# GpSimd takes six of the sixteen products with B, at the head of a tile, in a Mamba and mixture-of-experts block

## The chip, the cores and the metric

One core of a Trainium2 chip. The metric is the device time of one execution in microseconds. The kernel before took 1973.01 us (median of 3 runs, 1966.05 to 1973.41).

## The reference

The input is four images of 256 channels and 24 x 24 pixels. Two layers follow one another. Each is x = x + mamba(norm(x)), then t = t + experts(norm(t)), where the experts are a top-2 mixture of eight. The change lies in the Mamba part alone, which is the same in both layers:

```python
u, z = split(seq @ in_proj_w.T)                     # 128 channels each
u  = silu(causal_conv4(u) + conv_b)
dt, B, C = split(u @ x_proj_w.T, [4, 20])           # B and C: 16 states each
dt = softplus(dt @ dt_proj_w.T + dt_proj_b)
h  = exp(dt * A) * h + (dt * u) * B                 # per channel and state, step by step along the sequence
y  = sum_over_states(h * C) + u * D
out = (y * silu(z)) @ out_proj_w.T
```

A sequence has 2304 pixels and a leading token.

## The kernel before

The Mamba stage works on 24 tiles of T = 384 steps of the sequence per layer, six to an image. 128 channels times 16 states are 2048 rows of 384. They are held as 16 slices `c` of 128 partitions. A slice holds 32 channels of four states (partition group n of 32 and k = c // 4 pick the state, g = c % 4 the quarter of the channels). The code's N is 16 and its Q is 4. The prediction calls slice c "scan c" and "decay c", and the four slices of one k "group k".

Per tile the five engines do this:

- SyncE (`send`) stores the tile's B and C rows (`L_bc`, 20 rows) and dt and dt*u (`L_dw`) to memory and reads them back spread over the partitions: `L_dwq` in four DMAs (L738), `L_cbq` in four DMAs (L743). Of the five rows of 384 in a partition of `L_cbq`, four are C for the groups 0 to 3, and the fifth is B for group 3.
- ScalarE (`decay`, L492) makes exp(dt*A) for each slice into one of three PSUM banks, so decay c can start when scan c-3 is done. In between it makes the next tiles' silus (L454, L460, each pair between two loads of the function table, L536 and L540) and the steps of softplus (L213 to L232) two tiles ahead.
- VectorE makes the product (dt*u)*B for two slices at once (`times_b`, L574), from `L_dwq` and a spread of B that TensorE has put into PSUM, and runs the scans (`scan`, L587, one hardware scan of 384 steps per slice). It also makes dt*u (L595), the gate (L602) and the residual (L607), and after each second tile copies the last state (L649).
- GpSimd multiplies h by C, a whole group at a time (`times_c`, L669, called hc below), and makes the product with B for group 3, from `L_cbq`, in two instructions (L678). It also makes one subtraction of the softplus (L661).
- TensorE sums hc over the states (L364), spreads B for groups 0 to 2 (L354), and makes the projections: u and z (L323, L330), dt (L340), B and C (L336), the output (L371).

The order on each engine is the order in which the code is written; there is no scheduler. Every engine works through its own list and waits on semaphores. On TensorE a tile's list is: the three adding matmuls of softplus (L344, L348, L350) and z for the next tile; sum of hc 3 of the tile before; u for the tile after next (L323); spread of B for group 2; u*D (L358); sum of hc 0; spread of B for the next tile; dt and B, C projections for the tile after next; sum of hc 1; output of the tile before; spread of B; sum of hc 2. On ScalarE the first two softplus steps for the tile after next (L213, L216) stand between decay 10 and decay 11, and wait for the projection L340. `L_hc` has room for two groups.

`tile_pairs` writes out the first and last pair of tiles and loops over the pairs between. A pair has an even tile (r = 0) and an odd one (r = 1).

Of the kernel before, what the change touches and what calls it, by code (L numbers as in the profile page):

```python
# [16 lines left out]
ALU = mybir.AluOpType  # L17
# [3 lines left out]
P = 128  # L21
# [5 lines left out]
T = 4 * PT  # L27
NT = TOK // PT
TPB = PIX // PT
N = 16  # L30
TAPS = 4
E = 8
Q = 4
QW = P // Q
QR = Q + 1
DA_RING = 3
# [200 lines left out]
def mamba(nc, m, L, wp):  # L237
# [14 lines left out]
    with ExitStack() as ctx:  # L252
        new = ctx.enter_context(semaphores(nc))

        def sb(name, shape, dt=F32):
            return ctx.enter_context(nc.sbuf_tensor(f"{L}_{name}", shape, dt))
# [24 lines left out]
        dwq = sb("dwq", [P, 2, Q, 2, T])  # L281
        dbu = sb("dbu", [P, 6, T])
        dbp = sb("dbp", [P, Q, T])
        h = sb("h", [P, N, T])
# [30 lines left out]
        def _(pe):  # L315
# [36 lines left out]
            def spread_b(t, r, k):  # L352
                wait(pe, sem["dbu"], 6 * t + 2 * k - 2)
                nc.tensor.matmul(b_ps(r, k), w_b[:, k, :], u[:, r, :], start=True, stop=True).then_inc(sem["b"], 1)  # L354
# [208 lines left out]
        def _(dve):  # L563
            def times_b(t, r, p, k, i):
                dve.wait_ge(sem["b"], 3 * t + k + 1)
                if k == 0 and i == 0:
                    dve.wait_ge(s_dw[r], 64 * (p + 1))
                q = 2 * k + i
                if q >= 3:
                    dve.wait_ge(sem["scan"], t * N + 2 * q - 4)  # L570
                else:
                    wait(dve, sem["scan"], (t - 1) * N + 2 * q + 8)
                at = 2 * (q % 3)
                nc.vector.tensor_tensor(dbu[:, at:at + 2, :], dwq[:, r, 2 * i:2 * i + 2, 1, :], spread(b_ps(r, k)),  # L574
                                        ALU.mult).then_inc(sem["dbu"], 1)

            def scan(t, c, slot):
                k, g = c // Q, c % Q
                dve.wait_ge(sem["da"], t * N + c + 1)
                if k < Q - 1:  # L580
                    dve.wait_ge(sem["dbu"], 6 * t + c // 2 + 1)
                else:
                    dve.wait_ge(sem["dbu_p"], 2 * t + g // 2 + 1)
                wait(dve, sem["hc"], Q * (t - 1) + k + 1)
                first = h[:, c, T - 1:T] if slot is None else carry[:, slot, c:c + 1] if isinstance(slot, int) \
                    else carry[:, bass.ds(slot, 1), c:c + 1].rearrange("p a n -> p (a n)")
                nc.vector.tensor_tensor_scan(h[:, c, :], da(t % 2 if isinstance(t, int) else int(slot is None), c),  # L587
                                             dbu[:, c % 6, :] if k < Q - 1 else dbp[:, g, :], first, ALU.mult, ALU.add
                                             ).then_inc(sem["scan"], 1)
# [35 lines left out]
            def tile(t, r, p, slot, last):  # L625
                for j in range(N // 2):
                    k, i = (j + 1) // 2, (j + 1) % 2
                    if k < Q - 1:
                        times_b(t, r, p, k, i)
                    elif j == N // 2 - 1 and not last:  # L630
                        times_b(t + 1, 1 - r, p + r, 0, 0)
                    scan(t, 2 * j, slot)
                    scan(t, 2 * j + 1, slot)
                    if j == 1 and not last:
                        times_u(t + 1, 1 - r, [(s_dw_row[r], 16 * (p + 1))])
                    if not (isinstance(t, int) and t == 0):
# [21 lines left out]
        def _(pool):  # L658
# [13 lines left out]

            def times_b(t, r, p, i):
                if i == 0:
                    pool.wait_ge(s_cb[r], 64 * (p + 1))
                    pool.wait_ge(s_dw[r], 64 * (p + 1))
                    wait(pool, sem["scan"], t * N)
                nc.gpsimd.tensor_tensor(dbp[:, 2 * i:2 * i + 2, :], dwq[:, r, 2 * i:2 * i + 2, 1, :],  # L678
                                        spread(cbq[:, r, Q, :]), ALU.mult).then_inc(sem["dbu_p"], 1)

# [18 lines left out]

            def tile(t, r, p, last):  # L700
                for k in range(Q):
                    times_c(t, r, p, k)
                    if k < 2:
                        times_b(t, r, p, k)
                    if k == 2 and not last:
                        lost(t + 2)
# [10 lines left out]
        def _(sp_):  # L717
# [4 lines left out]
            def send(t, r, p):  # L722
                gone, there = count(64 * p), count(16 * (p + 1))
                bc_out, dt_out, w = count(t + 1), count(t + 1), count(t + 1)
                decayed, driven, mixed, driven_p = count((t - 1) * N), count((t - 1) * 6), count((t - 1) * Q), count((t - 1) * 2)
                sp_.wait_ge(sem["bc_out"], bc_out)
# [625 lines left out]
def pack(np, g):  # L1352
# [71 lines left out]
```

## Time and profile before

| | |
|---|---|
| median of 3 runs | 1973.01 us |
| profiled execution | 1973.6 us |
| its span | 1971.8 us |
| TensorE / VectorE / GpSimd / ScalarE busy | 73% / 69% / 58% / 47% of the span |
| mean granted clock of TensorE | 0.878 of full |

The profile is of one execution. Times are in microseconds from the start of its span. In a row of the timeline the first number is the start, the second how long the instructions of the row lasted from first start to last end; a number in brackets is the idle time ahead of it on its engine and what ended it. Matmul ends are modelled. Since an instruction's write-back lies beside the start of the next, the step from one start to the next is a little shorter than the duration. PE is TensorE, DVE VectorE, ACT ScalarE, POOL GpSimd, SPq SyncE's DMA queue. The scans of the first Mamba stage run from about 50 to 550, those of the second from about 1060 to 1600. The rows come from one even tile (413.90 to 436.3) and the odd one behind it (436.3 to 457.7), which have no irregular wait.

### The profile page before, as it was taken

Reading aid. Unit: us, or ns where it says so; the run is one execution under the profiler, and the core shown is the slowest. Engines: PE = TensorE matmul, PEld = TensorE weight load, DVE = VectorE, ACT = ScalarE, POOL = GpSimd, SP = SyncE. Lnnn points to the kernel's source line nnn. Section 1 sums busy time; section 2 is a strip of 40 time slices with the busy share of each in tenths; the row PEclk is TensorE's granted clock in tenths of the full one; section 3 lists DMA queues with packets and bytes.
Section 4 is the critical chain, followed back from the end, with each engine's and each line's share of the span. In section 5 each row is a group of like instructions: output and inputs, shape, how many; then the busy total and the mean of one; then the engine's idle time right before and its main releaser. Section 6 shows DMA issues by size and latency. Waiting matters only on the chain. (4 is left out here: it accounts for less than half of the span.)

```text
span 1971.8 us, 28551 instructions
## 1 busy us (share of the span) xinstructions
PE 1445.4 (73%) x7776; PEld 980.9 (50%) x7777; DVE 1359.6 (69%) x1913; ACT 928.1 (47%) x1695; POOL 1138.6 (58%) x788
## 2 busy tenths in 40 slices
PE   6666766667656599999956766666667662799993
PEld 4333333333314499999834333333333222799992
DVE  2899999999995422222143999999999967444443
ACT  6666677667743011111136666677666731011111
POOL 0687788888880244444302888888878850355540
PEclk9889898998968699999968788998998866899996
DMA  3655566555638110111034565566555634111114
GB/s 110 147 135 121 129 144 146 125 126 134 145 79 354 54 41 32 38 37 36 26 126 98 129 138 121 129 143 139 134 121 135 148 136 188 38 48 48 47 41 152
DMA packets 75964, 217.61 MB, mean 110 GB/s; under 512 B 11856, under 2 KB 27408, under 8 KB 72592
## 3 DMA queue, kind: packets, MB, share of 16 engines
q1 hardware_dynamic: 67664, 194.53, 38.9%
q0 software_dynamic: 8256, 22.56, 3.5%
q8 instruction: 20, 0.33, 0.1%
q14 instruction: 24, 0.20, 0.0%
HBM read 178.34 MB, written 38.70 MB: 110 GB/s over the span
## 5 line engine op out<-in xcount | busy, mean ns | idle before, releaser
L669 POOL TENSOR_TENSOR L_hc<-L_h,L_cbq 128x1536 f32<-128x1536 f32 x192 | 660.1, 3438 | 210.6 <-DVE L_h L587 207.5
L492 ACT ACTIVATE ps<-L_dwq,L_negA 128x384 f32<-128x384 f32 x768 | 426.7, 574 | 227.4 <-DVE L_h L587 215.5
L364 PE MATMUL ps<-L_hc,same 128*32 128x384 f32 x1536 | 190.0, 571 | 238.9 <-POOL L_hc L669 238.9
L574 DVE TENSOR_TENSOR L_dbu<-L_dwq,ps 128x768 f32<-128x768 f32 x288 | 270.7, 941 | 29.4 <-DVE L_carry L649 13.1
L587 DVE TENSOR_TENSOR_SCAN L_h<-ps,L_h,L_dbu 128x384 f32<-128x384 f32 x288 | 275.0, 1002 | 12.9 <-ACT ps L492 12.8
L587 DVE TENSOR_TENSOR_SCAN L_h<-ps,L_carry,L_dbu 128x384 f32<-128x384 f32 x288 | 274.2, 1001 | 6.5 <-DVE L_dbu L574 4.7
L364 PEld LDWEIGHTS ps<-L_hc,same 128*32 128x32 f32 x1536 | 31.5, 113 | 358.2 <-POOL L_hc L669 324.3
L1151 DVE COPY Xn<-L_w 128x2048 f32 x86 | 107.6, 1253 | 117.1 <-PE ps L1101 108.3
L1134 ACT ACTIVATE L0e_hT<-ps 128x512 f32<-128x512 f32 x86 | 51.3, 597 | 267.2 <-PE ps L1101 267.2
L678 POOL TENSOR_TENSOR L_dbp<-L_dwq,L_cbq 128x768 f32<-128x768 f32 x96 | 175.1, 1824 | 0.0
L323 PE MATMUL ps<-Xn,L_fold 128*128 (+1 forms) x480 | 103.3, 368 | 89.2 <-DVE L_dw L595 89.2
L1101 PE MATMUL ps<-L0e_xT,Xn 128*128 128x128 f32 x1376 | 159.1, 277 | 3.2 <-DVE Xn L1151 3.2
L1101 PEld LDWEIGHTS ps<-L0e_xT,Xn 128*128 128x128 f32 x1376 | 158.8, 194 | 4.7 <-issue 3.6
L1101 PE MATMUL ps<-L1e_xT,Xn 128*128 128x128 f32 x1376 | 159.1, 277 | 2.6 <-DVE Xn L1151 2.6
L1101 PEld LDWEIGHTS ps<-L1e_xT,Xn 128*128 128x128 f32 x1376 | 158.3, 194 | 4.6 <-issue 3.2
L1116 PE MATMUL ps<-L_w,L0e_hT 128*128 x688 | 152.3, 380 | 0.9 <-ACT L0e_hT L1134 0.9
L323 PEld LDWEIGHTS ps<-Xn,L_fold 128*128 128x128 f32 x480 | 87.7, 211 | 120.0 <-issue 102.5
L354 PE MATMUL ps<-L_u,L_wp 128*128 128x384 f32 x288 | 141.9, 579 | 0.0
L1116 PEld LDWEIGHTS ps<-L_w,L0e_hT 128*128 128x128 f32 x688 | 129.4, 191 | 17.3 <-issue 1.1
L1134 ACT ACTIVATE L1e_gl<-ps 128x512 f32<-128x512 f32 x43 | 25.7, 597 | 217.7 <-PE ps L1101 217.7
L661 POOL TENSOR_TENSOR L_sp_a<-L_sp_e,L_sp_g 128x384 f32<-128x384 f32 x48 | 48.3, 1006 | 123.1 <-ACT L_sp_g L228 123.1
L1039 POOL TENSOR_TENSOR L0e_give_done<-ones 128x1 f32<-128x1 f32 x44 | 8.5, 192 | 164.1 <-DVE L0e_yt L1173 162.3
(278 smaller groups left out, 2301.4 us busy)
## 6 DMA issues: line engine op xcount, KB each, us to landing
L_dwq<-dw_rows SPq DMA_DIRECT2D x192, 384.0 KB, 6.2
L_cbq<-cb_rows SPq DMA_DIRECT2D x192, 240.0 KB, 9.9
dw_rows<-L_dw SPq DMA_DIRECT2D x48, 384.0 KB, 2.3
L_w<-in_up SPq DMA_DIRECT2D x16, 1024.0 KB, 11.7
L_w<-in_down SPq DMA_DIRECT2D x8, 1024.0 KB, 26.6
tok_rows<-Xn SPq DMA_DIRECT2D x6, 768.0 KB, 13.1
L0s_got<-results SPq DMA_DIRECT2D x18, 256.0 KB, 2.9
L1s_got<-results SPq DMA_DIRECT2D x18, 256.0 KB, 3.5
```

What stands on the lines that cost most here:

```text
L323: mm = nc.tensor.matmul(ua_ps[:, j * (T // 2):(j + 1) * (T // 2)], fold[:, g, :], column(t, img, back), start=(k in (0, 2)), stop=(k in (1 ...
L354: nc.tensor.matmul(b_ps(r, k), w_b[:, k, :], u[:, r, :], start=True, stop=True).then_inc(sem["b"], 1)
L364: mm = nc.tensor.matmul(y_ps[g * QW:(g + 1) * QW, :], same[:, 0:QW], hc[:, (k % 2) * Q + g, :], start=False, stop=(k == Q - 1))
L492: nc.scalar.activation(da(r, c), dwq[:, r, c % Q, 0, :], ACT.Exp, scale=negA[:, 0, c:c + 1]).then_inc(sem["da"], 1)
L574: nc.vector.tensor_tensor(dbu[:, at:at + 2, :], dwq[:, r, 2 * i:2 * i + 2, 1, :], spread(b_ps(r, k)), ALU.mult).then_inc(sem["dbu"], 1)
L587: nc.vector.tensor_tensor_scan(h[:, c, :], da(t % 2 if isinstance(t, int) else int(slot is None), c), dbu[:, c % 6, :] if k < Q - 1 else d ...
L669: nc.gpsimd.tensor_tensor(hc[:, at:at + Q, :], h[:, Q * k:Q * k + Q, :], cbq[:, r, k, :].unsqueeze(1).to_broadcast([P, Q, T]), ALU.mult).t ...
L678: nc.gpsimd.tensor_tensor(dbp[:, 2 * i:2 * i + 2, :], dwq[:, r, 2 * i:2 * i + 2, 1, :], spread(cbq[:, r, Q, :]), ALU.mult).then_inc(sem["d ...
L1101: mm = nc.tensor.matmul(ps[:, h * NBH + b, (f % BF) * TS:(f % BF + 1) * TS], w1_t[:, h, i, f * P:(f + 1) * P], xT[:, r, i, h, :], start=(i ...
L1116: mm = nc.tensor.matmul(ps[:, 7, h * D:(h + 1) * D], hT[:, r, h, f, :], w2[:, bass.ds(e[h], 1), f, :].rearrange("p e d -> p (e d)"), start ...
L1134: nc.scalar.activation(dst, ps[:, h * NBH + b, :], ACT.Silu if gated else ACT.Gelu).then_inc(sem["act"], 1)
L1151: nc.vector.tensor_copy(w1_t[:, h].rearrange("p i f -> p (i f)"), w1[:, bass.ds(e, 1)].rearrange("p e i f -> p (e i f)")).then_inc(sem["st ...
```

## The change

GpSimd makes six products with B instead of four: those of the slices 10 to 15. B for group 2 is sent through the spread by DMA too, so `L_cbq` has six rows, `L_bc` 24. VectorE makes the ten others in five instructions, which stand where they stood; the sixth, for the slices 10 and 11, is gone. GpSimd's products are one of 768 columns (slices 10 and 11) and one of 1536 (12 to 15), and both stand at the head of the tile, ahead of `times_c` for group 0; before, there were two of 768 behind groups 0 and 1. `L_dbu` has ten rows instead of six and is no longer used in rotation, `L_dbp` has six instead of four.

```diff
-QR = Q + 1
+QR = Q + 2
...
-        dbu = sb("dbu", [P, 6, T])
-        dbp = sb("dbp", [P, Q, T])
+        dbu = sb("dbu", [P, 10, T])
+        dbp = sb("dbp", [P, 6, T])
...
             def spread_b(t, r, k):
-                wait(pe, sem["dbu"], 6 * t + 2 * k - 2)
+                wait(pe, sem["dbu"], 5 * t + (-1, 0, 2)[k])
...
-                q = 2 * k + i
-                if q >= 3:
-                    dve.wait_ge(sem["scan"], t * N + 2 * q - 4)
-                else:
-                    wait(dve, sem["scan"], (t - 1) * N + 2 * q + 8)
-                at = 2 * (q % 3)
+                at = 4 * k + 2 * i
+                wait(dve, sem["scan"], (t - 1) * N + at + 2)
...
-                if k < Q - 1:
-                    dve.wait_ge(sem["dbu"], 6 * t + c // 2 + 1)
+                if c < 10:
+                    dve.wait_ge(sem["dbu"], 5 * t + c // 2 + 1)
                 else:
-                    dve.wait_ge(sem["dbu_p"], 2 * t + g // 2 + 1)
+                    dve.wait_ge(sem["dbu_p"], 2 * t + (1 if c < 12 else 2))
...
             def tile(t, r, p, slot, last):
                 for j in range(N // 2):
                     k, i = (j + 1) // 2, (j + 1) % 2
-                    if k < Q - 1:
+                    if 2 * k + i < 5:
                         times_b(t, r, p, k, i)
...
-            def times_b(t, r, p, i):
-                if i == 0:
-                    pool.wait_ge(s_cb[r], 64 * (p + 1))
-                    pool.wait_ge(s_dw[r], 64 * (p + 1))
-                    wait(pool, sem["scan"], t * N)
-                nc.gpsimd.tensor_tensor(dbp[:, 2 * i:2 * i + 2, :], dwq[:, r, 2 * i:2 * i + 2, 1, :],
-                                        spread(cbq[:, r, Q, :]), ALU.mult).then_inc(sem["dbu_p"], 1)
+            def times_b2(t, r, p):
+                pool.wait_ge(s_cb[r], 64 * (p + 1))
+                pool.wait_ge(s_dw[r], 64 * (p + 1))
+                wait(pool, sem["scan"], (t - 1) * N + 12)
+                nc.gpsimd.tensor_tensor(dbp[:, 0:2, :], dwq[:, r, 2:4, 1, :], spread(cbq[:, r, Q + 1, :]), ALU.mult
+                                        ).then_inc(sem["dbu_p"], 1)
+
+            def times_b3(t, r):
+                wait(pool, sem["scan"], t * N)
+                nc.gpsimd.tensor_tensor(dbp[:, 2:6, :], dwq[:, r, :, 1, :],
+                                        cbq[:, r, Q, :].unsqueeze(1).to_broadcast([P, Q, T]), ALU.mult
+                                        ).then_inc(sem["dbu_p"], 1)
...
             def tile(t, r, p, last):
+                times_b2(t, r, p)
+                times_b3(t, r)
                 for k in range(Q):
                     times_c(t, r, p, k)
-                    if k < 2:
-                        times_b(t, r, p, k)
                     if k == 2 and not last:
                         lost(t + 2)
```

GpSimd's list for the first two tiles of a layer, before. `L_dbp` is the product with B, `L_hc` that with C, `L_sp_a` the subtraction:

```order
15 L669 TENSOR_TENSOR L_hc<-L_h,L_cbq 128x1536 [waits L0_scan,L0_cb_spread0]
16 L678 TENSOR_TENSOR L_dbp<-L_dwq,L_cbq 128x768 [waits L0_dw_spread0,L0_cb_spread0]
17 L669 TENSOR_TENSOR L_hc<-L_h,L_cbq 128x1536 [waits L0_scan]
18 L678 TENSOR_TENSOR L_dbp<-L_dwq,L_cbq 128x768
19 L669 TENSOR_TENSOR L_hc<-L_h,L_cbq 128x1536 [waits L0_scan,L0_y]
20 L661 TENSOR_TENSOR L_sp_a<-L_sp_e,L_sp_g 128x384 [waits L0_g]
21 L669 TENSOR_TENSOR L_hc<-L_h,L_cbq 128x1536 [waits L0_scan,L0_y]
22 L669 TENSOR_TENSOR L_hc<-L_h,L_cbq 128x1536 [waits L0_scan,L0_y,L0_cb_spread1]
23 L678 TENSOR_TENSOR L_dbp<-L_dwq,L_cbq 128x768 [waits L0_scan,L0_dw_spread1,L0_cb_spread1]
24 L669 TENSOR_TENSOR L_hc<-L_h,L_cbq 128x1536 [waits L0_scan,L0_y]
```

and the same place now (L665 was L669, L673 and L678 are the new products):

```order
15 L673 TENSOR_TENSOR L_dbp<-L_dwq,L_cbq 128x768 [waits L0_dw_spread0,L0_cb_spread0]
16 L678 TENSOR_TENSOR L_dbp<-L_dwq,L_cbq 128x1536
17 L665 TENSOR_TENSOR L_hc<-L_h,L_cbq 128x1536 [waits L0_scan,L0_cb_spread0]
18 L665 TENSOR_TENSOR L_hc<-L_h,L_cbq 128x1536 [waits L0_scan]
19 L665 TENSOR_TENSOR L_hc<-L_h,L_cbq 128x1536 [waits L0_scan,L0_y]
20 L657 TENSOR_TENSOR L_sp_a<-L_sp_e,L_sp_g 128x384 [waits L0_g]
21 L665 TENSOR_TENSOR L_hc<-L_h,L_cbq 128x1536 [waits L0_scan,L0_y]
22 L673 TENSOR_TENSOR L_dbp<-L_dwq,L_cbq 128x768 [waits L0_scan,L0_dw_spread1,L0_cb_spread1]
23 L678 TENSOR_TENSOR L_dbp<-L_dwq,L_cbq 128x1536 [waits L0_scan]
24 L665 TENSOR_TENSOR L_hc<-L_h,L_cbq 128x1536 [waits L0_scan,L0_y,L0_cb_spread1]
```

Both products moved ahead of hc 0 of their tile, and so directly behind hc 3 of the tile before.

VectorE's list from the gate (L602) of an odd tile to the copy of the last state, before (`L_yz` is the gate, a scan is printed as SCALAR_TENSOR_TENSOR):

```order
54 L602 TENSOR_TENSOR L_yz<-L_zs,ps 128x384
55 L574 TENSOR_TENSOR L_dbu<-L_dwq,ps 128x768
56 L587 SCALAR_TENSOR_TENSOR L_h<-ps,L_h,L_dbu 128x384 x2
57 L574 TENSOR_TENSOR L_dbu<-L_dwq,ps 128x768
58 L587 SCALAR_TENSOR_TENSOR L_h<-ps,L_h,L_dbu 128x384 x4
59 L587 SCALAR_TENSOR_TENSOR L_h<-ps,L_h,L_dbp 128x384 x2
60 L607 TENSOR_TENSOR X<-X,ps 128x2x96
```

and now:

```order
52 L598 TENSOR_TENSOR L_yz<-L_zs,ps 128x384
53 L570 TENSOR_TENSOR L_dbu<-L_dwq,ps 128x768
54 L583 SCALAR_TENSOR_TENSOR L_h<-ps,L_h,L_dbu 128x384 x4
55 L583 SCALAR_TENSOR_TENSOR L_h<-ps,L_h,L_dbp 128x384 x4
56 L603 TENSOR_TENSOR X<-X,ps 128x2x96
```

The product between scan 7 and scan 8 is gone, and the scans 10 and 11 read GpSimd's buffer. The lists of TensorE and ScalarE keep their order; the projection and the copy of B and C have 24 rows instead of 20.

## Rows read from the trace of the kernel before

**Rows 1.** The page: busy us of each engine, share of the span, instructions.

```profile
PE 1445.4 (73%) x7776; PEld 980.9 (50%) x7777; DVE 1359.6 (69%) x1913; ACT 928.1 (47%) x1695; POOL 1138.6 (58%) x788
```

**Rows 2.** Windows of two tiles: us, busy PE, PEld, DVE, ACT, POOL, clock, DMA.

```profile
413.90:436.30 22.40, 16.57 (x73) 8.12 (x70) 21.41 (x28) 16.19 (x29) 18.24 (x7) 0.86 0.58 133
436.30:457.70 21.40, 13.27 (x69) 6.33 (x69) 21.15 (x26) 15.22 (x27) 18.26 (x7) 1.00 0.62 139
```

**Rows 3.** Waits of VectorE, whole span: us in total, times, longest.

```profile
DVE L_h L587 <- ACT ps L492: 14.6, 31, 1.9
...
DVE L_dbu L574 <- PE ps L354: 10.3, 7, 2.1
```

**Rows 4.** Timeline of VectorE in the odd tile: start, us, instruction.

```profile
442.97 1.92 DVE L587 TENSOR_TENSOR_SCAN L_h<-ps,L_h,L_dbu 128x384 f32<-128x384 f32 x2
...
445.25 0.94 DVE L574 TENSOR_TENSOR L_dbu<-L_dwq,ps 128x768 f32<-128x768 f32 x1
446.12 1.91 DVE L587 TENSOR_TENSOR_SCAN L_h<-ps,L_h,L_dbu 128x384 f32<-128x384 f32 x2
447.95 0.93 DVE L574 TENSOR_TENSOR L_dbu<-L_dwq,ps 128x768 f32<-128x768 f32 x1
449.13 3.74 DVE L587 TENSOR_TENSOR_SCAN L_h<-ps,L_h,L_dbu 128x384 f32<-128x384 f32 x4 [0.25 <-ACT ps L492]
452.84 1.92 DVE L587 TENSOR_TENSOR_SCAN L_h<-ps,L_h,L_dbp 128x384 f32<-128x384 f32 x2
```

**Rows 5.** Timeline of ScalarE in the odd tile.

```profile
444.01 0.58 ACT L492 ACTIVATE ps<-L_dwq,L_negA 128x384 f32<-128x384 f32 x1 [1.71 <-DVE L_h L587]
444.62 1.28 ACT L536 ACT_TABLE_LOAD   x1
...
448.34 1.59 ACT L492 ACTIVATE ps<-L_dwq,L_negA 128x384 f32<-128x384 f32 x3
449.87 0.56 ACT L213 ACTIVATE L_sp_a<-ps,L_wp 128x384 f32<-128x384 f32 x1
...
452.07 0.57 ACT L492 ACTIVATE ps<-L_dwq,L_negA 128x384 f32<-128x384 f32 x1
```

**Rows 6.** Timeline of GpSimd in the odd tile.

```profile
436.40 3.44 POOL L669 TENSOR_TENSOR L_hc<-L_h,L_cbq 128x1536 f32<-128x1536 f32 x1 [0.17 <-DVE L_h L587]
441.76 3.45 POOL L669 TENSOR_TENSOR L_hc<-L_h,L_cbq 128x1536 f32<-128x1536 f32 x1 [1.92 <-DVE L_h L587]
445.16 1.84 POOL L678 TENSOR_TENSOR L_dbp<-L_dwq,L_cbq 128x768 f32<-128x768 f32 x1
...
451.51 1.84 POOL L678 TENSOR_TENSOR L_dbp<-L_dwq,L_cbq 128x768 f32<-128x768 f32 x1
453.30 3.43 POOL L669 TENSOR_TENSOR L_hc<-L_h,L_cbq 128x1536 f32<-128x1536 f32 x1
```

**Rows 7.** Timeline of TensorE in the odd tile.

```profile
446.23 0.85 PE L364 MATMUL ps<-L_hc,same 128*32 128x384 f32 x8
447.01 0.91 PE L354 MATMUL ps<-L_u,L_wp 128*128 128x384 f32 x2
447.76 0.81 PE L340 MATMUL ps<-L_u,L_w_dt 128*128 128x384 f32 x2
...
451.60 0.85 PE L364 MATMUL ps<-L_hc,same 128*32 128x384 f32 x8 [2.28 <-POOL L_hc L669]
```

**Rows 8.** Timeline of GpSimd and ScalarE in the even tile.

```profile
413.98 3.43 POOL L669 TENSOR_TENSOR L_hc<-L_h,L_cbq 128x1536 f32<-128x1536 f32 x1
...
428.36 0.56 ACT L213 ACTIVATE L_sp_a<-ps,L_wp 128x384 f32<-128x384 f32 x1
```

**Rows 9.** Timeline of TensorE in another tile, as its clock falls.

```profile
1382.69 1.40 PE L364 MATMUL ps<-L_hc,same 128*32 128x384 f32 x8 [2.80 <-POOL L_hc L669]
1384.03 1.65 PE L344 MATMUL ps<-L_sp_r,ident 128*128 128x384 f32 x2
```

**Rows 10.** The page: DMA issues, KB each, median us from issue to landing.

```profile
L_cbq<-cb_rows SPq DMA_DIRECT2D x192, 240.0 KB, 9.9
```

**Rows 11.** Timeline of SyncE's queue in the odd tile.

```profile
446.39 1.77 SPq L743 DMA_DIRECT2D L_cbq<-cb_rows  x4
```

More of the change, by code:

```diff
@@ L577, in scan @@
             def scan(t, c, slot):
-                k, g = c // Q, c % Q
+                k = c // Q
                 dve.wait_ge(sem["da"], t * N + c + 1)
-                if k < Q - 1:
-                    dve.wait_ge(sem["dbu"], 6 * t + c // 2 + 1)
+                if c < 10:
+                    dve.wait_ge(sem["dbu"], 5 * t + c // 2 + 1)
                 else:
-                    dve.wait_ge(sem["dbu_p"], 2 * t + g // 2 + 1)
+                    dve.wait_ge(sem["dbu_p"], 2 * t + (1 if c < 12 else 2))
                 wait(dve, sem["hc"], Q * (t - 1) + k + 1)
@@ L587, in scan @@
                 nc.vector.tensor_tensor_scan(h[:, c, :], da(t % 2 if isinstance(t, int) else int(slot is None), c),
-                                             dbu[:, c % 6, :] if k < Q - 1 else dbp[:, g, :], first, ALU.mult, ALU.add
+                                             dbu[:, c, :] if c < 10 else dbp[:, c - 10, :], first, ALU.mult, ALU.add
                                              ).then_inc(sem["scan"], 1)
@@ L724, in send @@
                 bc_out, dt_out, w = count(t + 1), count(t + 1), count(t + 1)
-                decayed, driven, mixed, driven_p = count((t - 1) * N), count((t - 1) * 6), count((t - 1) * Q), count((t - 1) * 2)
+                decayed, driven, mixed, driven_p = count((t - 1) * N), count((t - 1) * 5), count((t - 1) * Q), count((t - 1) * 2)
                 sp_.wait_ge(sem["bc_out"], bc_out)
@@ L1370, in pack @@
     state = g("x_proj_w")[4:].reshape(2, Q, Q, P)
-    put("bc", np.concatenate([state[1].transpose(1, 0, 2), state[0, Q - 1][:, None]], 1).reshape(Q * QR, P).T)
+    put("bc", np.concatenate([state[1].transpose(1, 0, 2), state[0, Q - 1][:, None], state[0, Q - 2][:, None]], 1).reshape(Q * QR, P).T)
     put("brep", np.repeat(state[0].reshape(N, P), QW, 0).T)
```

## The prediction

> **What bounds the kernel now.** I first read the busy shares of the page and then two neighbouring tiles of the stretch that the diff touches. VectorE (DVE) is busy 69% of the span and GpSimd (POOL) 58% [rows 1]; inside a tile of the state scan VectorE has work for 21.4 of 22.4 us (an even tile) or 21.2 of 21.4 us (an odd one) [rows 2]. That looks like a stage in which each VectorE instruction costs its full time. The list of waits corrects this: in the scans VectorE waits 31 times for ScalarE (ACT) and 7 times in the products for TensorE (PE), 14.6 and 10.3 us together [rows 3]. So I laid the instructions of one odd tile side by side, engine by engine [rows 4 to 7]. I call its states 0 to 15, "scan 8" the scan of state 8, "decay 8" ScalarE's exp for it, "group k" the four states 4k to 4k+3, and "hc k" GpSimd's product of h with C for group k.
>
> What is to be seen there: scan 8 starts at 449.13, and the product that stands ahead of it started at 447.95 and lasts 0.93. Instructions of VectorE that need not wait follow a product after about 0.86 us (scans 6 and 7 start 0.87 after their product started at 445.25), so scan 8 could have started at 448.81; the row puts 0.25 us on ScalarE [rows 4]. On ScalarE decay 7 starts at 444.01, when scan 4 has freed its bank, and then follow without a gap two table loads of 1.28 with two silus between them, and decay 8 at 448.34 [rows 5]. Scan 4 started at 442.97. From scan 4 to scan 8 there are therefore 6.16 us that belong to ScalarE, whatever VectorE does between. After scan 8 ScalarE has no gap either: the first softplus step (L213) at 449.87, decay 12 from 452.07 to 452.64, and scan 12 starts at 452.84, 0.20 after it.
>
> **The change on VectorE: one product less, worth nothing.** The removed instruction is the product of 128x768 just ahead of scan 8, 48 in all, 0.86 us of its time each. Were all of it on the path, 48 x 0.86 = 41.3 us would go. But VectorE then stands ready for scan 8 at 447.95, and decay 8 still comes at 448.34, so scan 8 starts at 449.13 as before: the wait grows from 0.3 to 1.2 us. The even tile has the same order on ScalarE. I take 0, with 0 and 41.3 as the two ends; 0 is what the nearest rows show.
>
> The Trainium skill ("Perfetto Trace Analysis", Identifying the Most-Contended Engine) tells to take the engine with the highest occupancy as the bottleneck and work on it first. By that rule the 41.3 us would come off. The row above speaks against it for this place; the rule stands as a rival below.
>
> **The change on GpSimd.** Before, its order in a tile was hc 0, product of 768, hc 1, product of 768, hc 2, subtraction (L661), hc 3. Now it is product of 768, product of 1536, hc 0, hc 1, hc 2, subtraction, hc 3. The product of 1536 is not in the trace: hc has its shape, with the same broadcast second input, and goes on after 3.40 us (441.76 to 445.16); two products of 768 would be 2 x 1.79 = 3.58. I take 3.40. Its work in a tile grows by 3.40 - 1.79 = 1.61 us to about 19.9 us [rows 2, 6], still under a tile's 21.4. What matters is where it stands. hc 3 of the tile before can start only when scan 15 is done, and both products now come behind it and ahead of hc 0. Odd tile: hc 3 starts at 436.40, + 3.40 + 1.79 + 3.40 puts hc 0 at 444.99, and its 3.45 end it at 448.44. Before it ended at 445.21 [rows 6]. Both new waits of the products (the spreads, and the scans of the last tile) are past by then, so the order alone makes this delay.
>
> **Who waits for hc 0.** TensorE's queue is in order. The sum over hc 0 (L364) stands ahead of the spread of B for the next tile, of the projection for dt (L340) and the one for B and C of the tile after. Before, that sum started at 446.23 and the projection for dt was done at 447.76 + 0.81 = 448.57, 2.34 us later [rows 7]. Now it starts at 448.44 + 0.05 = 448.49 and the projection is done at 450.83. ScalarE had L213 at 449.87 in its order, 1.30 us of cover; now it starts at 450.87, and that is 1.00 us late. Behind it on ScalarE are decays 11 to 15, and VectorE waits for those. The whole run to decay 12 moves by 1.00, so scan 12 comes at 453.84. VectorE alone is there earlier: scans 8 to 11 end at 452.84 if nothing holds them [rows 4], and scan 11 is held by less than the 1.0 us, as decay 11 had some lead. So ScalarE decides, and the end of the tile, and with it the next hc 3, is 1.00 later. Odd tile: 21.40 + 1.00 = 22.40 us.
>
> Even tile: hc 3 starts at 413.98 [rows 8], + 12.04 is 426.02, the sum at 426.07, the projection done at 428.41, L213 at 428.45 instead of 428.36: 0.09 late. It has the carry's copy at its head, which is why the same chain just fits. Both kinds of tile end up bound by one loop: scan 15, hc 3, two products, hc 0, sum, spread, projection, softplus, decay 12, scan 12 to 15.
>
> Sum: the chain exists where a tile t+2 follows, 11 odd and 11 even tiles in each of two layers. 22 x 1.00 = +22.0; 22 x 0.09 = +2.0. Against it: of the waits in [rows 3] about 22 x 0.25 = 5.5 us are the regular one before scan 8; the other 19.4 come in single tiles, which the list doesn't place. Where they fall in an odd tile, up to 1.0 us each is swallowed by the new wait; hc 2, no longer behind a product (451.51 to 453.30), starts when scan 11 ends and saves the even tiles up to 0.3 each. I take -5 for both (0 to -12).
>
> **TensorE's clock.** It was granted 0.86 in the even tile and 1.00 in the odd one [rows 2]; 0.86 is a mix of 2.4 and 1.2 GHz. Groups of matmuls at the higher level last 0.85 (L364) and 0.91 (L354, like L344 two passes of 384 columns) [rows 7]; at the lower 1.40 and 1.65 [rows 9]. If the chain ran at the lower one, its three groups would cost 0.55 + 0.74 + 0.74 = 2.0 us more. Until now ScalarE's 1.30 us of cover stood before that. Now the sum, which came straight behind the matmul before it, has an idle of 448.49 - 446.23 = 2.3 us ahead of it in an odd tile; the fall in [rows 9] came behind an idle of 2.80. If the lower level met the chain by its mean share ((0.28 + 0) / 2 = 0.14) it would cost 44 x 0.14 x 2.0 = 12 us. I take half, +6, as the new idle is the shorter one; ends 0 and, in all odd tiles, 22 x 2.0 = 44.
>
> **The spread of C and B.** Six rows of 384 in place of five go through four DMAs: 240 to 288 KB each. They now have to be there for the product that follows hc 3, not for hc 0. The first is issued at 446.39, the last about 1.3 later, and they land in 9.9 us (median) [rows 10, 11]: 457.6; a fifth more is 459.6. The product wants them at 458.71 + 0.08 + 3.40 = 462.2. Cover 2.6 us, cost 0; the storing of 24 in place of 20 rows and the copy of 24 partitions cost nothing that the rows could show. The larger buffers free VectorE's product from a wait that never ended last.
>
> Total: 1971.8 span in a run of 1973.6 us; + 22 + 2 - 5 + 6 = +25, so 1998.6. The median of the runs shown is 1973.0, 0.6 less than the profiled run: 1998.
>
> **The rivals.**
> - *Slower still, the clock:* the chain runs at 1.2 GHz in nearly all odd tiles. +24 - 5 + 44 = +63: 2036. For: the new idle lies just ahead of the chain. Against: in the odd tile an idle of 2.28 us is followed by a group of 0.85 [rows 7].
> - *No change:* hc 0 comes late but is hidden, because the two products or the chain are faster than I add up. It needs 1.0 us out of 14.4; the sizes come from repeating rows, so I give it little. 1972, with the small gain of hc 2.
> - *Faster, the product was on the path:* VectorE's occupancy decides. Place: scan 8; it pays 0.86 a tile from the point at which decay 8 is done before VectorE asks for it. Then 1973 - 41 = 1932, or some 1950 with part of the delay of hc 0. Against: the 0.25 us wait in [rows 4], and ScalarE without a gap in [rows 5]. It is what the rule of the Trainium skill above would make of this change.
> - *Late spread:* landings 2.6 us later than I add up hold GpSimd at a tile's head and then the same chain: with 1 us in every tile +44 more, 2040.
>
> **How the numbers follow.** Mine 0.60, the clock 0.17, no change 0.13, faster 0.06, late spread 0.04. This kernel's measurement tells 0.5% (10 us) from no change. Slower by more than that: 0.60 + 0.17 + 0.04, less 0.03 for my own case coming out small, 0.78; within 0.5%: 0.13 + 0.02 = 0.15; faster 0.07. The range runs from the no-change case to the clock case, 1972 to 2034: about 0.08 lies below and 0.10 above.
>
> **What would show it.** Right: scans (L583 now) waiting about 1.2 us for ScalarE before scan 8 in each tile, a second wait of 0.7 to 1.0 us before scans 11 and 12 in odd tiles, odd tiles of 22.4 us, ScalarE waiting for TensorE's projection before L213, GpSimd going from hc 3 through both products into hc 0 without idle. Wrong: odd tiles at 21.4 or less, scan 8 less than 6.1 us behind scan 4, or GpSimd waiting at the head of a tile for the spread.

## The result and the profile after

The kernel after takes 2017.56 us (median of 4 runs, 2013.30 to 2020.63), 1.023 of the kernel before (95% interval 1.0209 to 1.0256). The forecast was 1998 in a range of 1972 to 2034. The sign and the mechanism came as forecast, the size is 44 us in place of 25. A few executions (two of e2, two of the kernel before beside e5 to e8) fell into a slower state of the chip; the ratios leave them out.

First the page of the kernel after: busy time of each engine, the costliest groups (time, mean ns | idle ahead), and the DMAs to landing.

```profile
PE 1458.6 (72%) x7776; PEld 984.3 (49%) x7777; DVE 1322.8 (66%) x1865; ACT 931.9 (46%) x1695; POOL 1215.6 (60%) x788
...
L678 POOL TENSOR_TENSOR L_dbp<-L_dwq,L_cbq 128x1536 f32<-128x1536 f32 x48 | 165.1, 3440 | 0.0
...
L_cbq<-cb_rows SPq DMA_DIRECT2D x192, 288.0 KB, 10.9
```

VectorE works 36.8 us less than in [rows 1] (48 instructions less), GpSimd 77.0 more, which is 1.60 in each of 48 tiles (forecast 1.61). The product of 1536 has a duration of 3.44 like hc, and no idle ahead of it. The landing went from 9.9 [rows 10] to 10.9, where I had put a fifth more, 11.9.

Next the waits of the kernel after over the whole span (us in total, times, longest), VectorE, ScalarE and GpSimd:

```profile
DVE L_h L583 <- ACT ps L492: 85.4, 96, 2.7
...
DVE L_dbu L570 <- PE ps L354: 17.5, 13, 1.6
...
ACT L_sp_a L213 <- PE ps L340: 41.4, 25, 3.0
...
POOL L_dbp L673 <- DMA L_cbq<-cb_rows: 18.4, 2, 9.5
```

The first row was 14.6 us and 31 times in [rows 3]. The third had no row before: ScalarE now waits for the projection of dt in 25 places. GpSimd waits for the spread only twice, for the first tile of each of the two stages.

This is an odd tile without disturbance (402.06 to 424.42), the timeline of VectorE, ScalarE, GpSimd and TensorE from top to bottom:

```profile
411.85 1.92 DVE L583 TENSOR_TENSOR_SCAN L_h<-ps,L_h,L_dbu 128x384 f32<-128x384 f32 x2
414.86 1.93 DVE L583 TENSOR_TENSOR_SCAN L_h<-ps,L_h,L_dbu 128x384 f32<-128x384 f32 x2 [1.08 <-ACT ps L492]
...
418.13 1.02 DVE L583 TENSOR_TENSOR_SCAN L_h<-ps,L_h,L_dbp 128x384 f32<-128x384 f32 x1 [0.44 <-ACT ps L492]
419.55 1.92 DVE L583 TENSOR_TENSOR_SCAN L_h<-ps,L_h,L_dbp 128x384 f32<-128x384 f32 x2 [0.40 <-ACT ps L492]
...
416.57 0.58 ACT L213 ACTIVATE L_sp_a<-ps,L_wp 128x384 f32<-128x384 f32 x1 [0.91 <-PE ps L340]
...
402.14 3.44 POOL L665 TENSOR_TENSOR L_hc<-L_h,L_cbq 128x1536 f32<-128x1536 f32 x1 [0.98 <-DVE L_h L583]
405.53 1.81 POOL L673 TENSOR_TENSOR L_dbp<-L_dwq,L_cbq 128x768 f32<-128x768 f32 x1
407.31 3.44 POOL L678 TENSOR_TENSOR L_dbp<-L_dwq,L_cbq 128x1536 f32<-128x1536 f32 x1
410.70 6.83 POOL L665 TENSOR_TENSOR L_hc<-L_h,L_cbq 128x1536 f32<-128x1536 f32 x2
...
414.19 0.85 PE L364 MATMUL ps<-L_hc,same 128*32 128x384 f32 x8 [2.15 <-POOL L_hc L665]
414.97 0.91 PE L354 MATMUL ps<-L_u,L_wp 128*128 128x384 f32 x2
415.72 0.81 PE L340 MATMUL ps<-L_u,L_w_dt 128*128 128x384 f32 x2
```

It is the loop of the prediction, link by link. hc 3 starts at 402.14, both products and hc 0 follow without idle, the sum over hc 0 starts 12.05 later (forecast 12.09), the projection ends 2.34 behind that, and L213 stands 14.43 behind hc 3 (forecast 14.47). Scan 8 waits 1.08 for ScalarE, scans 11 and 12 wait 0.84 together. The tile takes 22.36 us; 22.40 was forecast.

But not every tile looks so. Measured from the end of one scan 15 to the next, the tiles 2 to 21 of the first stage run, but for the first of them, in a pattern of four: 24.20, 22.37, 22.48, 23.11. In the second stage the same values come in a longer, less even order, with 24.0 as a fifth. Of the 20 odd tiles in these two stretches 8 take 22.36, 7 take 23.1 and 5 take 24.0. Of the floor values the forecast has two (22.49 even, 22.40 odd); the other two are new. These windows of the kernel after are the undisturbed odd tile, an odd one of 23.1, an even one of 24.2 and, in the second stage, an odd one of 24.0 (us, busy PE, PEld, DVE, ACT, POOL, granted clock, DMA share, GB/s):

```profile
402.06:424.42 22.36, 13.36 (x67) 6.16 (x66) 20.44 (x24) 15.49 (x27) 19.81 (x7) 0.97 0.64 142
446.91:470.02 23.11, 16.98 (x71) 8.09 (x70) 20.54 (x24) 15.21 (x27) 19.82 (x7) 0.85 0.64 143
470.02:494.22 24.20, 16.47 (x69) 8.85 (x69) 20.73 (x26) 16.48 (x29) 19.84 (x7) 0.86 0.58 132
1438.12:1462.14 24.02, 16.82 (x73) 7.85 (x70) 20.49 (x25) 15.20 (x27) 19.82 (x7) 0.86 0.60 133
```

VectorE, ScalarE and GpSimd have the same work in each odd tile. What differs is TensorE's clock. Its timeline in the three disturbed tiles, and the instruction that waits for it:

```profile
459.06 0.85 PE L364 MATMUL ps<-L_hc,same 128*32 128x384 f32 x8 [2.05 <-POOL L_hc L665]
459.84 1.01 PE L354 MATMUL ps<-L_u,L_wp 128*128 128x384 f32 x2
460.64 1.49 PE L340 MATMUL ps<-L_u,L_w_dt 128*128 128x384 f32 x2
...
462.16 0.58 ACT L213 ACTIVATE L_sp_a<-ps,L_wp 128x384 f32<-128x384 f32 x1 [1.54 <-PE ps L340]
...
477.21 3.22 PE L323 MATMUL ps<-Xn,L_fold 128*128 x10 [2.77 <-DVE L_dw L591]
...
481.55 0.95 DVE L570 TENSOR_TENSOR L_dbu<-L_dwq,ps 128x768 f32<-128x768 f32 x1 [1.56 <-PE ps L354]
...
1450.27 1.45 PE L364 MATMUL ps<-L_hc,same 128*32 128x384 f32 x8 [2.11 <-POOL L_hc L665]
1451.65 1.65 PE L354 MATMUL ps<-L_u,L_wp 128*128 128x384 f32 x2
1453.09 1.17 PE L340 MATMUL ps<-L_u,L_w_dt 128*128 128x384 f32 x2
...
1454.30 0.58 ACT L213 ACTIVATE L_sp_a<-ps,L_wp 128x384 f32<-128x384 f32 x1 [2.52 <-PE ps L340]
```

In the first the clock falls from 2.4 to 1.2 GHz inside the chain, and the projection takes 1.49 in place of 0.81. In the last it falls with the chain's first group, and L213 comes 1.67 us later than in an undisturbed tile. In the even tile it is u's matmuls (L323) that run slowly: the spread of B behind them is late, and VectorE's product ahead of scan 6 waits 1.56 for it.

Call the time of an undisturbed tile its floor: 21.39 (odd) and 22.42 us (even) in the kernel before, 22.37 and 22.48 in the one after. Over the 40 tiles 2 to 21 of both stages, what exceeds the floors is 15.4 us in the kernel before and 30.5 in the one after. The span grew by 42.3 in the profiled runs: 36 in these 40 tiles, 3.7 in the first two tiles of the stages and 2.6 in the last two.

The last tile of each stage prepares no further tile, and so has no chain through L213. Yet it takes 20.88 instead of 20.13. There VectorE's residual waits for the output's matmuls (L371), which stand behind the sum over hc 1, and GpSimd ends hc 1 there 15.37 us behind the start of hc 3, 14.62 in the kernel before:

```profile
602.99 0.35 DVE L603 TENSOR_TENSOR X<-X,ps 128x192 f32<-128x192 f32 x1 [2.05 <-PE ps L371]
```

### The profile page after: what moved, and what is told of

It reads as the page before. It is cut to its first block and busy times, and to the rows that moved or that the text cites. A ratio compares the mean times of both kernels' runs of the same rounds, so it can differ in the third digit from the quotient of the medians.

```text
span 2014.2 us, 28471 instructions
## 1 busy us (share of the span) xinstructions
PE 1458.6 (72%) x7776; PEld 984.3 (49%) x7777; DVE 1322.8 (66%) x1865; ACT 931.9 (46%) x1695; POOL 1215.6 (60%) x788
## 5 line engine op out<-in xcount | busy, mean ns | idle before, releaser
L665 POOL TENSOR_TENSOR L_hc<-L_h,L_cbq 128x1536 f32<-128x1536 f32 x192 | 659.1, 3439 | 158.7 <-DVE L_h L583 158.0
L364 PE MATMUL ps<-L_hc,same 128*32 128x384 f32 x1536 | 206.2, 589 | 248.7 <-POOL L_hc L665 248.1
L570 DVE TENSOR_TENSOR L_dbu<-L_dwq,ps 128x768 f32<-128x768 f32 x240 | 226.2, 943 | 35.8 <-PE ps L354 17.5
L583 DVE TENSOR_TENSOR_SCAN L_h<-ps,L_h,L_dbu 128x384 f32<-128x384 f32 x240 | 231.4, 1004 | 23.9 <-ACT ps L492 23.4
L583 DVE TENSOR_TENSOR_SCAN L_h<-ps,L_carry,L_dbu 128x384 f32<-128x384 f32 x240 | 230.5, 1002 | 22.3 <-ACT ps L492 22.3
L364 PEld LDWEIGHTS ps<-L_hc,same 128*32 128x32 f32 x1536 | 36.4, 115 | 363.0 <-POOL L_hc L665 351.0
L323 PE MATMUL ps<-Xn,L_fold 128*128 (+1 forms) x480 | 108.2, 381 | 98.9 <-DVE L_dw L591 98.9
L678 POOL TENSOR_TENSOR L_dbp<-L_dwq,L_cbq 128x1536 f32<-128x1536 f32 x48 | 165.1, 3440 | 0.0
L583 DVE TENSOR_TENSOR_SCAN L_h<-ps,L_h,L_dbp 128x384 f32<-128x384 f32 x144 | 140.1, 1003 | 33.6 <-ACT ps L492 33.6
L323 PEld LDWEIGHTS ps<-Xn,L_fold 128*128 128x128 f32 x480 | 91.5, 218 | 129.8 <-issue 112.7
L583 DVE TENSOR_TENSOR_SCAN L_h<-ps,L_carry,L_dbp 128x384 f32<-128x384 f32 x144 | 136.9, 999 | 6.3 <-ACT ps L492 6.1
## 6 DMA issues: line engine op xcount, KB each, us to landing
L_cbq<-cb_rows SPq DMA_DIRECT2D x192, 288.0 KB, 10.9
```

The source lines that it names most:

```text
L323: mm = nc.tensor.matmul(ua_ps[:, j * (T // 2):(j + 1) * (T // 2)], fold[:, g, :], column(t, img, back), start=(k in (0, 2)), stop=(k in (1 ...
L364: mm = nc.tensor.matmul(y_ps[g * QW:(g + 1) * QW, :], same[:, 0:QW], hc[:, (k % 2) * Q + g, :], start=False, stop=(k == Q - 1))
L665: nc.gpsimd.tensor_tensor(hc[:, at:at + Q, :], h[:, Q * k:Q * k + Q, :], cbq[:, r, k, :].unsqueeze(1).to_broadcast([P, Q, T]), ALU.mult).t ...
L678: nc.gpsimd.tensor_tensor(dbp[:, 2:6, :], dwq[:, r, :, 1, :], cbq[:, r, Q, :].unsqueeze(1).to_broadcast([P, Q, T]), ALU.mult).then_inc(sem ...
```

## The experiments

Where fillers are named, they are matmuls of 128x128 on the identity matrix, put into TensorE's list ahead of a wait, that write into a part of a PSUM bank that nobody reads (the five ahead of z into one that z's matmuls then write anew); "0/6/7/6" are their numbers ahead of the sums over hc 0, hc 1, hc 2 and hc 3. In those kernels z's matmuls also move from ahead of the sum over hc 3 to behind it; no kernel has only this move, so what the fillers are said to do is done by both together.

### Is the removed product worth nothing?

e2 is the kernel before without VectorE's sixth product, and nothing else; scans 10 and 11 read what an earlier product left. e3 is the kernel after with that product put back, and nobody reads it.

The line that decides, in e2 and then in e3 (the counts of the semaphores go with it):

```diff
-                    if k < Q - 1:
+                    if 2 * k + i < 5:
                         times_b(t, r, p, k, i)
```

```diff
-                    if 2 * k + i < 5:
+                    if 2 * k + i < 6:
                         times_b(t, r, p, k, i)
```

> The kernel before, with VectorE's product for slices 10 and 11 left out and nothing in its place: scans 10 and 11 read what an older product left in that buffer. GpSimd, the spread and the orders are as before. My theory: scan 8 comes 6.16 us after scan 4 as ScalarE sets it, so the time stays within 0.5% of before, 1963 to 1975. Rival (VectorE's occupancy decides): 48 x 0.86 = 41 us less, 1932.

> The changed kernel, in which VectorE still makes the sixth product ahead of scan 8, into a buffer that nobody reads (dbu has twelve rows). My theory: it fills the wait for decay 8 and costs nothing, 2010 to 2025, with the wait before scan 8 back from about 1.2 to about 0.3 us. Rival (a product of VectorE costs its time): 2017 + 41 = 2058.

e2: 1973.77 us, ratio 0.9997 (0.9987 to 1.0008). e3: 2014.63, against 2017.56 of the kernel after: it costs nothing there either. A row each of VectorE's waits and timeline in e2, and one of the timeline in e3:

```profile
DVE L_h L587 <- ACT ps L492: 47.9, 48, 1.3
...
451.15 3.74 DVE L587 TENSOR_TENSOR_SCAN L_h<-ps,L_h,L_dbu 128x384 f32<-128x384 f32 x4 [1.10 <-ACT ps L492]
...
415.85 1.92 DVE L583 TENSOR_TENSOR_SCAN L_h<-ps,L_h,L_dbu 128x384 f32<-128x384 f32 x2 [0.23 <-ACT ps L492]
```

Of the 48 waits in e2's row 46 stand ahead of scan 8, one in each tile but the last of a stage, where ScalarE loads no tables. The median idle ahead of scan 8 went from 0.26 in the kernel before to 1.10 us, and in e3 it is back at 0.23. The time from scan 4 to scan 8 is 6.16 us, as before. A removed instruction that took 0.86 us of VectorE's time turned into a wait of nearly the same length. Step one is shown.

### Is it the order on GpSimd?

e1 is the kernel after with the product of 1536 behind hc 0 instead of ahead of it.

```diff
-                times_b3(t, r)
...
+                    if k == 0:
+                        times_b3(t, r)
```

> The changed kernel with only the place of GpSimd's second product moved: product of 768 at the head of a tile, then hc 0, then the product of 1536, then hc 1. Work on every engine is as in the changed kernel. My theory (place): hc 0 starts again when scan 3 ends, 5.4 us into an odd tile and 6.4 into an even one, the projection for dt is back under ScalarE's cover, scan 8 still waits some 1.2 us for decay 8. Undisturbed tiles 21.4 and 22.4 us as in the kernel before, time 1960 to 1980. Rival 1 (the amount of GpSimd's work, or the larger spread, costs): stays at 2005 to 2020. Rival 2 (VectorE's product was on the path and only the late hc 0 hid the gain): 1925 to 1940.

1990.56 us, ratio 1.0087 (1.0063 to 1.0110). Against the kernel after it gains 27 us, and the undisturbed odd tiles are back at 21.38 to 21.39, so the late hc 0 is what made them 1.0 us longer. But 1960 to 1980 was expected, and the usual even tile takes 23.0, not 22.4. TensorE and VectorE in an even tile of e1:

```profile
434.75 1.51 PE L364 MATMUL ps<-L_hc,same 128*32 128x384 f32 x8 [2.74 <-POOL L_hc L665]
436.19 1.65 PE L371 MATMUL ps<-L_yz,L_wp 128*128 128x192 f32 x4
...
437.99 0.35 DVE L603 TENSOR_TENSOR X<-X,ps 128x192 f32 x1 [0.43 <-PE ps L371]
```

hc 1 is now the late one. TensorE idles 2.74 ahead of its sum, the clock falls there, and the output's matmuls at 1.2 GHz (1.65 in place of 0.95, in all 20 even tiles of the 40) hold VectorE's residual.

### Does hc 0 act through ScalarE's queue?

e4 leaves GpSimd as in the kernel after and moves the first softplus steps (L213, L216) and those that follow one decay later in ScalarE's list.

```diff
-                    if c == 10:
+                    if c == 11:
                         dt_head(t + 2)
-                    if c == 11:
+                    if c == 12:
                         steps(t + 2)[2]()
...
-                    if c == 12:
+                    if c == 13:
                         steps(t + 2)[3]()
```

> The changed kernel with ScalarE's softplus steps for the tile after next one decay later: L213 and L216 behind decay 11 instead of decay 10, the others moved along. My theory: decay 11 no longer stands behind the late projection, and L213 has 0.6 us more cover, so the undisturbed odd tile falls from 22.4 to about 21.5 to 21.8 us and the time to 1980 to 2005. Rival (the late hc 0 acts on another way than through ScalarE's queue, say through the sums or the residual): 2010 to 2025, unchanged.

2023.89 us, ratio 1.0242 (1.0218 to 1.0267): a miss, in the range of the rival. The tiles show why. Two neighbours of e4 as windows, then TensorE and VectorE in the first, and two rows of VectorE's waits:

```profile
432.70:457.40 24.70, 15.72 (x64) 8.33 (x63) 21.02 (x25) 16.45 (x30) 19.80 (x8) 0.79 0.58 129
457.40:478.70 21.30, 12.99 (x68) 6.12 (x67) 19.93 (x25) 15.44 (x28) 19.83 (x8) 1.00 0.64 144
...
439.46 3.56 PE L323 MATMUL ps<-Xn,L_fold 128*128 x10 [2.83 <-DVE L_dw L591]
...
444.41 0.95 DVE L570 TENSOR_TENSOR L_dbu<-L_dwq,ps 128x768 f32<-128x768 f32 x1 [2.23 <-PE ps L354]
...
DVE L_dbu L570 <- PE ps L354: 56.8, 32, 2.2
...
DVE L_h L583 <- ACT ps L492: 54.5, 55, 1.8
```

An undisturbed odd tile takes 21.30, less than in the kernel before, with GpSimd still late. That speaks for the theory, but only 5 of the 20 odd tiles are undisturbed. In all 20 even tiles u's matmuls take longer than the 1.89 us that they take at the high clock (L323, 2.39 to 3.56), the product behind them waits up to 2.2 us, and the even tiles average 24.3. Against the kernel after, an odd tile is 0.3 us shorter on average and an even one 1.0 longer. From here on the clock was the question.

### How much is the late hc 0, how much the clock?

e5 is the kernel after with the fillers 4/0/6/6, e6 the kernel before with 0/6/7/6, e7 is e1 with 0/6/7/6. The edit, as in e5:

```diff
+            def fill(n):
+                for _ in range(n):
+                    nc.tensor.matmul(ps[:, 5, T:T + P], ident[:], ident[:], start=False, stop=False)
...
-                    z_in(t + 1, img1)
+                    if first:
+                        z_in(t + 1, img1)
                 if not first:
+                    fill(6)
                     sum_y(t - 1, 1 - r, Q - 1)
+                    if more:
+                        z_in(t + 1, img1)
...
+                fill(4)
                 sum_y(t, r, 0)
...
+                fill(6)
                 sum_y(t, r, 2)
```

> The changed kernel with TensorE kept busy: filler matmuls (identity times identity, 128 columns, into unread columns of the bank of y) ahead of the sums over hc 0 (4), hc 2 (6) and hc 3 (6), and the matmuls for z moved behind the sum over hc 3. Nothing that others wait for is added elsewhere. My theory: the profile after has undisturbed tiles of 22.36 (odd) and 22.48 us (even), and the others are 0.7 to 1.7 us longer because TensorE is granted 1.2 GHz in the run from the sum over hc 0 to the projection for dt, or in u's matmuls; with the clock held all tiles are near 22.4 and the time falls by some 35 us to 1978 to 1990. Rival (the longer tiles come from the spread or from GpSimd): unchanged, 2010 to 2025. Rival (fillers only delay the queue): slower than 2017.

> The kernel before with the same kind of fillers: 6 ahead of the sum over hc 1, 7 ahead of hc 2, 6 ahead of hc 3, and z moved the same way. My theory: its undisturbed tiles are 21.39 and 22.42 us, its mean 22.37; with the clock held about 20 us go, 1950 to 1960. The gap between this run and the changed kernel with fillers is then the pure cost of the late hc 0, 22 x 1.0 = 22 us plus a few. Rival: the fillers do nothing here, 1965 to 1978.

> GpSimd's order of e1 (product of 768, hc 0, product of 1536, hc 1) with the fillers of e6. In e1 the odd tiles were 21.38 us, as I expected, but the even ones 23.0: hc 1 starts 0.45 us later there, TensorE idles 2.7 us ahead of its sum and the output projection runs at the lower clock, so the residual comes late. My theory: with the clock held the even tiles are 22.4 again and the time is that of the kernel before with fillers, 1948 to 1960. Rival (the later hc 1 costs by itself): 1970 to 1985.

e5: 1988.03 us (1.0082, 1.0054 to 1.0110). e6: 1968.36 (0.9972, 0.9955 to 0.9989). e7: 1966.02 (0.9968, 0.9954 to 0.9983). Windows of e5, an odd and an even tile (the cuts are to 0.1 us):

```profile
396.00:418.40 22.40, 17.71 (x102) 10.69 (x103) 20.45 (x25) 15.32 (x28) 19.83 (x7) 1.00 0.68 149
418.40:440.90 22.50, 16.74 (x100) 10.05 (x100) 20.56 (x26) 16.43 (x30) 19.87 (x7) 1.00 0.61 138
```

In e5 all 20 odd tiles among the 40 take 22.37 to 22.39: matmuls with no use, and the move of z, took 29.5 us off the kernel after. The excess over the floors fell from 30.5 to 6.5 us, with no edit to GpSimd or to the spread, so nearly all that lay above the floors was TensorE's. e5 less e6 is 19.7 us, where the forecast has 24 for the late hc 0. It is not a clean price: e6 still has 11.9 us above its floors, 5.4 more than e5. By the floors alone the late hc 0 costs 20.8 us in the 40 tiles. e6 and e7 missed, 8 and 6 us above their ranges, and e6 lies in the range of its rival. Their odd tiles are at 21.39, all but one in each, but every second even tile still takes 23.5.

### Is the larger spread free?

e8 is the kernel before with only the sixth row in the spread, which nobody reads.

```diff
-QR = Q + 1
+QR = Q + 2
```

> The kernel before with only the sixth row in the spread: the projection of 24 rows, the copy of 24, four DMAs of 288 KB instead of 240 KB; the extra row is read by nobody. My theory: hidden, 1968 to 1980. Rival (the larger transfers hold dwq, cbq or GpSimd): 0.3 us or more a tile, 1988 or more.

1976.26 us, ratio 1.0015 (1.0001 to 1.0028): in the range of the theory, at most 5.5 us, 3 by the middle of the interval. I had taken 0.

### With the clock held, what are the orders worth?

e9 is e7 with five more fillers ahead of z's matmuls. e10 is the kernel before with the same fillers as e9. e11 is GpSimd's order of the kernel after, L213 one decay later (e4's edit), fillers 4/0/6/6 and the five.

```diff
+                    if more:
+                        fill(5, 7)
+                        z_in(t + 1, img1)
```

> The kernel of e7 (product of 768, hc 0, product of 1536, hc 1, with fillers) with five more fillers between the sum over hc 3 and z, in the bank that z is about to take. In e5, e6 and e7 all undisturbed odd tiles hold their floor, and what is left are even tiles of 23.5 instead of 22.4 us, in which u's matmuls (L323) run at the lower clock behind an idle of 2.0 us. My theory: these go to 22.4 too, 20 x 0.5 = some 10 us, 1952 to 1960, ratio to before 0.990 to 0.994. Rival (these tiles wait for something else): 1962 to 1970, as e7.

> The kernel before with the same five further fillers. If GpSimd's sixth product is worth nothing even in the better place and with the clock held, this equals e9 within 0.3%, 1952 to 1962. Rival (with the clock held VectorE's product is on the path): e9 is 20 us or more below this one.

> The changed kernel with GpSimd's order as it is (both products ahead of hc 0), with L213 and L216 one decay later as in e4, and with the fillers. In e4 undisturbed odd tiles were 21.30 us, but most tiles were disturbed by TensorE's clock. My theory (hc 0 acts through ScalarE's queue alone): with the clock held odd tiles are 21.3 to 21.5, even ones 22.4, time 1950 to 1966, where e5 took 1988. Rival (it also acts on another way): 1975 or more.

e9: 1958.86 us (0.9925, 0.9908 to 0.9943). e10: 1959.29 (0.9926, 0.9908 to 0.9943). e11: 1956.27 (0.9912, 0.9890 to 0.9934). All three as expected, and all three faster than both kernels. VectorE's waits ahead of scans in e10 (a short wait of scan 8 can be listed under the product ahead of it, as in the second row), and then in e9:

```profile
DVE L_h L599 <- ACT ps L504: 6.2, 22, 0.8
...
DVE L_h L599 <- DVE L_dbu L586: 5.8, 19, 0.3
```

```profile
DVE L_h L595 <- ACT ps L504: 50.6, 46, 1.5
```

e10 has the sixth product on VectorE and e9 has not; the waits grow from 12.0 to 50.6 us, 0.84 in each of 46 tiles, and the time is the same. So taking the product off VectorE stays worthless even where nearly every tile is at its floor. And ScalarE's wait for the projection, in e5 and then in e11:

```profile
ACT L_sp_a L213 <- PE ps L340: 23.1, 26, 1.1
```

```profile
ACT L_sp_a L213 <- PE ps L340: 0.7, 2, 0.3
```

e11 has hc 0 as late as the kernel after, and odd tiles of 21.31 to 21.35, all but one. e5's odd tiles were at their floor of 22.37 without the five further fillers, so this 1.0 us is the step's place in ScalarE's list, and e4's theory is shown once the clock is held: in the tiles 2 to 21 the late hc 0 costs only where an early place in ScalarE's list waits for it. Of the 32 us between the times of e5 and e11 this is some 20; the rest are the tiles above their floors and the ends of the stages.

### Does ScalarE's chain hold the tile?

e12 is e9 without the two table loads of a tile; both silus become the identity, so u and z are not activated.

```diff
-                        nc.scalar.preload_act_table_set(SILU)
-                        silu_z(t + 1, 1 - r)
+                        silu_z(t + 1, 1 - r, ACT.Identity)
```

> The kernel e9 (VectorE's product gone, GpSimd's second product behind hc 0, fillers) with ScalarE's two table loads between decay 7 and decay 8 left out; to allow that, the silus of u and z inside the tiles are replaced by the identity, so the output is another one. My theory: the 6.16 us from scan 4 to scan 8 are ScalarE's, 2.6 of them table loads; without them VectorE's list is the bound and the removed product pays at last: 0.3 + 0.86 = about 1.2 us a tile less than e9 in both kinds of tile, scan 4 to scan 8 about 5.0 us, time 1900 to 1920. Rival (another chain, GpSimd's or TensorE's, sits right behind): 1935 to 1958.

1934.79 us, ratio 0.9811 (0.9794 to 0.9828). From scan 4 to scan 8 it is 4.98 us, as expected, 1.2 less. Yet the tile gains less than half of that, by the medians of the 40 tiles: 21.39 to 20.99 odd, 22.45 to 21.90 even; 24 us in all. Rows of VectorE's waits in e12:

```profile
DVE X L613 <- PE ps L375: 24.2, 47, 2.3
...
DVE L_dbu L580 <- DMA L_dwq<-dw_rows: 13.9, 27, 2.6
```

VectorE's list of waits has no row for ScalarE in the scans any more. Whether the product taken off VectorE pays here is not shown: this kernel with the product was not run. But now the residual waits for the output, which comes behind the sum over hc 1, and GpSimd runs hc 0, the product of 1536 and hc 1 back to back. The time lies 0.2 us below the rival's range and 15 above the theory's: the theory had the way from scan 4 to scan 8 right, and the rival that another chain sits right behind.

## Why the prediction was right, and where its size was off

- *The product ahead of scan 8 is worth 0.* Right: e2 0.9997, e3 no cost, e9 and e10 equal. The rival in which it was on the path is excluded. That rival is what one would forecast here by the rule of the Trainium skill ("Perfetto Trace Analysis", Identifying the Most-Contended Engine) to work first on the engine with the highest occupancy. The trace decides: 36.8 us less work on VectorE, no time less.
- *GpSimd's order puts the end of hc 0 12.04 us behind the start of hc 3.* Right to 0.1 us, with no idle between.
- *Sum, spread, projection, L213, decay 12, scan 12.* Right: L213 at 14.43 behind hc 3, odd tile 22.36 (forecast 22.40), even tile 22.48 (22.49). By the floors this is 22 x 0.98 + 22 x 0.06 = 22.9 us; the forecast had 24.0.
- *The -5 for waits that the new one would swallow.* Half right, and outweighed. Of the 14.6 us in [rows 3] 9.2 stand ahead of scan 3, in ten tiles. They come from TensorE at 1.2 GHz: in all ten the softplus matmuls L344, L348 and L350 run at it in whole or in part, and ScalarE and then VectorE wait for them, as in this tile of the kernel before, where they last 1.65, 1.49 and 1.49 us:

```profile
218.54 0.58 ACT L473 ACTIVATE L_dw<-ps,L_ln_one 128x384 f32<-128x384 f32 x1 [4.18 <-PE ps L350]
...
219.63 1.02 DVE L587 TENSOR_TENSOR_SCAN L_h<-ps,L_h,L_dbu 128x384 f32<-128x384 f32 x1 [1.44 <-ACT ps L492]
```

  In the kernel after 0.5 us of these are left; whether the new wait swallowed them or the low clock no longer fell there was not separated. Irregular waits of the same origin, in the chain and behind u's matmuls, took more than they gave back.
- *The clock, +6.* This is the mis-sized term. With the -5 it stood at +1; measured is the excess over the floors, 30.5 - 15.4 = +15.1 us in the 40 tiles. A further 4.2 fell in the first and last tiles (6.3 less 2.1 for the chain in tiles 0 and 1). Of these 1.5 are a wait that the forecast did not have: the residual's in the last tile of each stage, 2.05 us there and 2.05 in e5 as well. It is the late hc 1 and no change of the clock, as the output runs at 1.2 GHz (1.65 us) in the last tile of both stages before, after and in e5. The other 2.7 were not traced to a cause. The 44 us of its upper end were for a low clock in all odd tiles. In my sum I multiplied the mean share of low clock (0.14) by the length of the chain. The mean did not change (0.878 before, 0.877 after); what changed is what stands in the low stretches and how much cover it has. And I counted the odd tile's chain only: the even tiles' u matmuls and the product behind them, 1.56 us late in the row above, were not in the sum. The even tiles carry 17.2 of the 30.5 us. The measured time lies midway between my own case (1998) and the rival with a low clock in nearly all odd tiles (2036): 12 of 20 odd tiles were disturbed. The range held because it reached to that rival, not because my sum was near.
- *The spread costs 0.* Nearly: e8 says 3 us, and GpSimd waits for it only at a stage's head. The late-spread rival is excluded.

What stays open: why the low clock falls in one tile and not in the next, and how much of the gain of e5 to e11 is the move of z's matmuls. The idle ahead of the sum over hc 0 was 2.15 us in the undisturbed tile and 2.11 in the one where the clock fell at once, so this idle alone does not decide it. Nor was it tried whether the 3 us of e8 are the larger transfer or the copy of 24 partitions.

## What to carry to other kernels

Before an instruction is taken off the busiest engine, ask whether the one behind it would have its operand any sooner; here it would not, and the work added elsewhere for it was all cost. When an in-order queue gets its operand later, follow everything that stands behind that wait down to the next engine's fixed place in its own list; a step moved one place later there gave the 1.0 us of an odd tile back, but the time gained only with TensorE's clock held (e11, not e4). In a pipeline that leaves TensorE gaps, read the tiles one by one, since a mean granted clock that stays the same can hide groups at half speed that have moved onto the path.

## What the runs showed of the hardware

- More matmuls can make the useful ones faster: the mean granted clock goes from 0.878 to 0.941 between the kernel before and one with 24 fillers a tile and z's matmuls moved (e10), and the time falls by 14 us, though TensorE is busy 1613.5 us in place of 1445.4. u's matmuls, up to 3.54 us before, take at most 1.89 in the 40 tiles.
- With no edit to TensorE's work at all, the position of 3.4 us of GpSimd work (the kernel after against e1) changed which tiles and which matmuls met 1.2 GHz: of the 20 even tiles 11 have u's matmuls slower than 1.89 us in the one and 6 in the other, and the output's take 1.65 in place of 0.95 in 6 and in all 20.
- A table load takes 1.28 us [rows 5], and the activation behind it follows within 0.03 us; taking both out of a tile shortens the way from scan 4 to scan 8 by 1.2 us, not by their 2.56, since VectorE's own list then fills it without a wait, and the tile by half a microsecond (e12), as other waits stood right behind.
